# Queries, keys and layer 1's first convolution as two streams in the two column halves of TensorE's array

## What is computed

```python
# layer 0, with xn = groupnorm(x), 32 groups
f = Wq @ xn + bq          # 32 x N        g = Wk @ xn + bk          # 32 x N
h = Wv @ xn + bv          # 256 x N
beta = softmax(f.T @ g, over the first index)
x = x + gamma * (h @ beta)
# layer 1, with xn = groupnorm(x)
y = bn_relu(w1 @ xn + b1)                 # 32 channels
packed = y[rows] * y[cols]                # all 528 pairs of channels
x = x + bn_relu(w2 @ packed + b2)         # 256 x N
```

## Time and profile before

| | us |
|---|---|
| median of 3 runs | 2307.71 (2307.48 to 2309.89) |
| the profiled execution | 2308.09 |
| its span | 2305.2 |

### The profile page before, as it was taken

One profiled execution on the slowest core, in us unless ns is written; L12 is line 12 of the kernel. 1 busy time (PEld: TensorE's weight loads), 2 busy tenths in 40 slices (PEclk: granted clock), 3 DMA queues, 4 the chain that ended last, 5 costly groups with the idle time before them and its releaser, 6 DMA issues.

```text
span 2305.2 us, 42586 instructions
## 1 busy us (share of the span) xinstructions
PE 2222.7 (96%) x16782; PEld 1637.3 (71%) x16782; DVE 1891.0 (82%) x3134; ACT 1671.3 (73%) x2691; POOL 631.0 (27%) x607
## 2 busy tenths in 40 slices
PE   2899999999999999999999999999999999999978
PEld 1477777777777777777777777777777777777733
DVE  6778888888788888888888888887978777787678
ACT  3477777777777777777777777777777777777856
POOL 2100111112222332332522233333432222221244
PEclk9999999999999999999999999999999999999999
DMA  4000000000012212211122112221101111111101
GB/s 175 24 1 1 1 8 8 8 17 1 9 44 70 70 54 61 65 42 42 47 70 70 47 55 54 65 67 45 52 15 43 35 34 33 29 33 34 33 24 64
DMA packets 56663, 95.20 MB, mean 41 GB/s; under 512 B 8016, under 2 KB 14864, under 8 KB 56464
## 3 DMA queue, kind: packets, MB, share of 16 engines
q1 hardware_dynamic: 56464, 92.49, 14.1%
HBM read 67.03 MB, written 19.14 MB: 37 GB/s over the span
## 4 chain that ended last, share of the span: by engine, by line
PE 91%; DVE 6%; ACT 1%; issue 1%; SPq 0%; DMA 0%; POOL 0%; DVEq 0%; ACTq 0%
PE acc L1392 19%; PE acc L1385 19%; PE acc L1386 19%; PE tps L1235 9%; PE sps L1251 9%; PE tps L1287 3%; PE acc L1229 3%; PE tps L1289 2%; PE tps L1273 1%; PE tps L1216 1%; PE tps L1266 1%; DVE xn L593 1%; DVE mx L623 1%; PE acc L1287 1%; DVE pl L642 1%
## 5 line engine op out<-in xcount | busy, mean ns | idle before, releaser
L1028 ACT ACTIVATE ph<-sps,esc 128x512 f16<-128x512 f32 x1024 | 703.7, 687 | 397.7 <-PE sps L1251 391.8
L1385 PE MATMUL acc<-hth,ph 128*128 128x257 f16 x4096 | 955.6, 274 | 3.2 <-ACT ot L1034 3.2
L1386 PE MATMUL acc<-htl,ph 128*128 128x256 f16 x4096 | 954.8, 273 | 0.0
L623 DVE TENSOR_REDUCE mx<-tps 128x1 f32<-128x512 f32 x1024 | 700.7, 686 | 302.3 <-PE tps L1235 298.1
L642 DVE TENSOR_TENSOR pl<-p,ph 128x512 f16<-128x512 f32 x1024 | 807.2, 788 | 39.5 <-ACT p L1029 38.4
L1029 ACT ACTIVATE p<-sps,esc 128x512 f32<-128x512 f32 x1024 | 700.1, 684 | 0.0
L1392 PE MATMUL acc<-hth,pl 128*128 128x257 f16 x4096 | 620.2, 273 | 0.0
L1392 PEld LDWEIGHTS acc<-hth,pl 128*128 128x128 f16 x4096 | 399.9, 98 | 159.4 <-issue 0.3
L1386 PEld LDWEIGHTS acc<-htl,ph 128*128 128x128 f16 x4096 | 401.0, 98 | 150.7 <-issue 0.3
L876 POOL TENSOR_TENSOR xl<-xn,xh 128x512 f16<-128x512 f32 x176 | 229.8, 1327 | 877.0 <-DVE xn L593 871.2
L1385 PEld LDWEIGHTS acc<-hth,ph 128*128 128x128 f16 x4096 | 401.2, 98 | 73.8 <-issue 4.6
(11 more groups left out here) (215 smaller groups left out, 1626.7 us busy)
## 6 DMA issues: line engine op xcount, KB each, us to landing
rt<-turned SPq DMA_DIRECT2D x96, 256.0 KB, 4.2
xt<-x SPq DMA_DIRECT2D x36, 512.0 KB, 3.7
xb<-x SPq DMA_DIRECT2D x32, 512.0 KB, 5.1
out<-zt SPq DMA_DIRECT2D x47, 256.0 KB, 2.0
rt<-turned SPq DMA_DIRECT2D x72, 64.0 KB, 4.7
turned<-yb SPq DMA_DIRECT2D x24, 96.0 KB, 1.9
out<-fst SPq DMA_DIRECT2D x8, 256.0 KB, 2.0
out<-htl SPq DMA_DIRECT2D x8, 256.0 KB, 2.0
```

The source lines that it names most:

```text
L623: V.reduce_max(mx[:, tile, c:c + 1], tps[par][:], AX).then_inc(t_free[par], 1)
L1028: A(ph[:, u % SLOTS], sps[u % 2][:], ACT.Exp, scale=esc[:]).then_inc(ph_ok, 1)
L1385: mm(acc[j][:, 0:C + 1], w, hth[:, t], start=(t == 0), stop=False)
L1386: mm(acc[j][:, 0:C], w, htl[:, t], start=False, stop=False)
```

## The change

For samples 1 to 3 (b >= 1) of the queries and keys, and for layer 1's n < 24, the six matmuls now have 64 weight columns instead of 128. Channel half 0 goes to partitions 0 to 63 of the bank and half 1 to partitions 64 to 127, alternating: two sums over half the channels each, for the same 512 pixels. The two halves have to be added:

- Queries and keys: ScalarE copies partitions 64 to 127 with the bias to float32 `qk_half` (`qk_part_out`), VectorE adds them into the bank (`qk_add`), ScalarE makes the high part from the sum (`qk_high`), VectorE the low part (`qk_low`). The sum has queries once and keys once, so `spread` repeats them with six transfers instead of five.
- Layer 1: ScalarE copies partitions 64 to 127 to the lower half of `yb0` (`y_part_out`), VectorE adds twice (`y_add`), once for partitions 0 to 63 and once for 64 to 127, the second behind a wait for the first; ScalarE's `y_out` works from `yb0` in place.

Places in the loop, before and after, for b >= 1: first queries and keys on TensorE t = 9 to 8, copy out in turn 10, add in turn 10, `qk_high` 11 to 12, `qk_low` 11 to 12. Second: TensorE t = 21 as before, copy out and add in turn 23, `qk_high` and `qk_low` 23 to 25. Layer 1's first convolution: t = 17 and 18 to 18 alone; copy out and adds in turn 20; `y_out` 20 to 22. `pairs` for half 0: t = 12, 13, 14 to 13, 14, 15; `z_out` 16 to 17. `transposed` t = 4 and 7 to 3 and 6, with `finish` and `second_stats` one turn earlier as well. For sample 0 the group stays at t = 0, the copy out and the add are in turn 1, `qk_high` goes from 2 to 3.

```diff
@@ SP
+                if b:
+                    sp.wait_ge(qk_hi, n + 1)
+                    for row in (0, 32):
+                        sp.dma_start(fst[row:row + 32, b % 2, at], qkh0[0:32]).then_inc(fg_in[par], 16)
+                    for row in (0, 64):
+                        sp.dma_start(gst[row:row + 32, keys_at(n)], qkh0[32:64]).then_inc(fg_in[par], 16)
+                    sp.wait_ge(qk_lo, n + 1)
+                    sp.dma_start(fst[64:96, b % 2, at], qkl0[0:32]).then_inc(fg_in[par], 16)
+                    sp.dma_start(gst[32:64, keys_at(n)], qkl0[32:64]).then_inc(fg_in[par], 16)
+                    return
@@ VectorE, setup
+            V.tensor_copy(bq2[2 * CK:3 * CK, :], bqk[0:CK, :])
+            over_stats(V.tensor_copy(bq2[3 * CK:4 * CK, :], bqk[3 * CK:4 * CK, :]))
@@ VectorE
+                if b:
+                    V.tensor_tensor(qkl0[0:64], bank[0:64], qkh0[0:64], ALU.subtract).then_inc(qk_lo, 1)
+                    return
+            def qk_add(b, c, bank):
+                dve.wait_ge(qk_part, (b - 1) * NCH + c + 1)
+                V.tensor_tensor(bank[0:64], bank[0:64], qk_half, ALU.add).then_inc(qk_sum, 1)
+            def y_add(n, bank):
+                dve.wait_ge(y_part, n + 1)
+                V.tensor_tensor(yb0[0:64], bank[0:64], yb0[64:128], ALU.add).then_inc(y_sum, 1)
+                dve.wait_ge(y_sum, 2 * n + 1)
+                V.tensor_tensor(yb0[64:128], bank[0:64], yb0[64:128], ALU.add).then_inc(y_sum, 1)
-                        if J and t in (5, 8):
-                            finish(G - 1, (t - 5) // 3, 1)
+                        if J and t in (back + 1, back + 4):
+                            finish(G - 1, (t - back - 1) // 3, 1)
+                        if nxt and t == (10 if b else 1):
+                            qk_add(b + 1, 2 * (J - 3), tps[1])
-                        if nxt and t == (11 if b else 3):
+                        if nxt and t == (12 if b else 3):
                             qk_low(b + 1, 2 * (J - 3), tps[1])
+                        if b and t == 20:
+                            y_add(n, tps[1])
@@ ScalarE
+                if b:
+                    act.wait_ge(qk_sum, n - NCH + 1)
+                    A(qkh0[0:64], bank[0:64], ACT.Copy).then_inc(qk_hi, 1)
+                    return
+            def qk_part_out(b, c, bank):
...
+                A(qk_half, bank[64:P], ACT.Identity, bias=bq2[64:P]).then_inc(qk_part, 1)
+            def y_part_out(n, bank):
+                act.wait_ge(y_mm, n + 1)
+                if n:
+                    act.wait_ge(qh_ok, 5 * n)
+                A(yb0[64:P], bank[64:P], ACT.Copy).then_inc(y_part, 1)
             def y_out(n, bank):
+                if n < SHARED:
+                    act.wait_ge(y_sum, 2 * n + 2)
+                    A(yb0[:], yb0[:], ACT.Relu, bias=t1a[:], scale=s1a[:]).then_inc(y_ok, 1)
+                    return
@@ TensorE
+                if b:
+                    for w, v in ((0, xh), (0, xl), (1, xh)):
+                        for i in range(H2):
+                            last = mm(bank[64 * i:64 * i + 64], wqkT[:, w, i, 32:96], v[:, k % RING, i],
+                                      start=(w == 0 and v is xh), stop=(w == 1))
+                    last.then_inc(qk_mm, 1)
+                    return
+            def project_y_halves(n, bank):
+                slot = JOB["second", n // NCH, n % NCH] % RING
+                for w, v in ((0, xh), (0, xl), (1, xh)):
+                    for i in range(H2):
+                        last = mm(bank[64 * i:64 * i + 64], w1T[:, w, i, 0:64], v[:, slot, i],
+                                  start=(w == 0 and v is xh), stop=(w == 1))
+                last.then_inc(y_mm, 1)
+                    back = 3 if b else 4
-                        if J and t in (4, 7):
+                        if J and t in (back, back + 3):
-                        if b and nxt and t == 9:
+                        if b and nxt and t == 8:
-                        if b and n >= 1 and t in (12, 13, 14):
+                        if b and n >= 1 and t in (13, 14, 15):
-                        if b and t in (17, 18):
-                            if t == 17:
...
+                        if b and t == 18:
...
+                            project_y_halves(n, tps[1])
```

More of the change, by code:

```diff
@@ L161, in build @@
         xh_ok, xn_ok, xl_ok = sem("xh_ok"), sem("xn_ok"), sem("xl_ok")
-        qk_mm, qk_hi, qk_lo = sem("qk_mm"), sem("qk_hi"), sem("qk_lo")
+        qk_mm, qk_part, qk_sum, qk_hi, qk_lo = sem("qk_mm"), sem("qk_part"), sem("qk_sum"), sem("qk_hi"), sem("qk_lo")
         fg_in = [sem("fg_in0"), sem("fg_in1")]
@@ L264, in spreads, with spread_before @@
         def spreads(b, c):
-            return 80 * (qk_turn(b, c) + 1)
+            turn = qk_turn(b, c) + 1
+            return 80 * min(turn, NCH // 2) + 96 * max(turn - NCH // 2, 0)
+        def spread_before(b, c):
+            turn = qk_turn(b, c)
+            return 80 * min(turn, NCH // 2) + 96 * max(turn - NCH // 2, 0)
         def keys_at(G):
@@ L780, in attend @@
                             normed(("qk", b + 1, 2 * (J - 3) + 1))
+                        if b and t == 20:
+                            y_add(n, tps[1])
                         if nxt and t == 23:
+                            qk_add(b + 1, 2 * (J - 3) + 1, tps[1])
+                        if nxt and t == 25:
                             qk_low(b + 1, 2 * (J - 3) + 1, tps[1])
@@ L1018, in value_high @@
                 A(hth[:, t:t + 2, 0:C], bank[:].rearrange("p (t c) -> p t c", t=2), ACT.Copy).then_inc(h_hi, 1)
+            def qk_part_out(b, c, bank):
+                n = b * NCH + c
+                act.wait_ge(qk_mm, n + 1)
+                if n > NCH:
+                    act.wait_ge(qk_sum, n - NCH)
+                else:
+                    act.wait_ge(fg_in[0], spread_before(b, c))
+                A(qk_half, bank[64:P], ACT.Identity, bias=bq2[64:P]).then_inc(qk_part, 1)
[4 more added lines that the diff above has]
+                A(yb0[64:P], bank[64:P], ACT.Copy).then_inc(y_part, 1)
             def row_copy(G, bank):
@@ L1102, in attend @@
                             product_high(n - 1, (3, 4, 6, 7, 8).index(t))
-                        if nxt and t == (11 if b else 2):
+                        if nxt and t == (12 if b else 3):
                             qk_high(b + 1, 2 * (J - 3), tps[1])
+                        if nxt and t == (10 if b else 1):
+                            qk_part_out(b + 1, 2 * (J - 3), tps[1])
+                        if b and t == 20:
+                            y_part_out(n, tps[1])
+                        if nxt and t == 23:
+                            qk_part_out(b + 1, 2 * (J - 3) + 1, tps[1])
                         if b and t == 12:
@@ L1108, in attend @@
                             high(("qk", b + 1, 2 * (J - 3) + 1))
-                        if b and n >= 1 and t == 16:
+                        if b and n >= 1 and t == 17:
                             z_out(n - 1, 0, tps[1])
-                        if b and t == 20:
+                        if b and t == 22:
                             y_out(n, tps[1])
-                        if nxt and t == 23:
+                        if nxt and t == 25:
                             qk_high(b + 1, 2 * (J - 3) + 1, tps[1])
@@ L1404, in attend @@
                                     pe.wait_ge(qk_lo, (b + 1) * NCH + 2 * (J - 3) + 1)
-                            for grp in ((0, 1), (2, 3), (4,))[t - 12]:
+                            for grp in ((0, 1), (2, 3), (4,))[t - 13]:
                                 pairs(n - 1, 0, grp, tps[1])
-                        if b and t in (17, 18):
-                            if t == 17:
-                                free(1)
-                                if n >= 1:
-                                    pe.wait_ge(z_ok, 2 * n - 1)
-                                pe.wait_ge(xl_ok, JOB["second", b - 1, J] + 1)
-                            project_y(n, t - 17, tps[1])
+                        if b and t == 18:
+                            free(1)
+                            if n >= 1:
+                                pe.wait_ge(z_ok, 2 * n - 1)
+                            pe.wait_ge(xl_ok, JOB["second", b - 1, J] + 1)
+                            project_y_halves(n, tps[1])
                         if nxt and t == 21:
                             if b:
-                                pe.wait_ge(y_ok, n + 1)
+                                pe.wait_ge(y_sum, 2 * n + 2)
                             pe.wait_ge(qk_lo, (b + 1) * NCH + 2 * (J - 3) + 1)
```

34 lines of the change are left out of this document (18 added, 16 removed).

## The result

The changed kernel takes 2333.77 us (median of 4 runs, 2330.14 to 2334.73) where the kernel before takes 2308.80 beside it: 1.0105 times as long, 95% interval 1.0087 to 1.0122. It is slower by 25.0 us. The profiled execution took 2333.31 us with a span of 2331.4, 26.2 longer than the span before.

A forecast was written before the change was run, and what follows sets the result against it. TensorE's streaming columns were taken as the bound, with nothing lost to waits within a chunk. Terms -31.0 + 9.6 + 16.3 + 5.8 + 4.6 + 4.3 + 0.8 + 0.3 = +10.7 gave 2318 us, 0.45% slower; range 2292 to 2334.

The forecast's parts named there:

- gain and switching: TensorE's 48 groups: two streams at once save 31.0 us; switching the array's shape costs 0.20 a group, 9.6 us.
- first queries and keys: Samples 1 and 2 running, chunks 3 to 6: step 13 loses 0.34 and 1.70 us, 8 times, +16.3 us.
- layer 1's sum: VectorE's two adds in turn 20 make maximum 20 late for piece 21, worse in chunks 2 and 7: +5.8 us.
- transposes earlier: Turns 4 and 7 get `ql` and `finish` together: 0.11 us lost twice in 21 chunks, +4.6 us.
- second convolution later: Moved from steps 12 to 14 to 13 to 15, so step 13 starts 1.30 us earlier: +4.3 us.
- sample 0's groups: Four groups ahead of the accumulators' first matmuls, now too short to cover TensorE's wait there: +0.8 us.
- setup and both ends: Forecast for setup only: two one-column copies on VectorE in front of TensorE's first transposes, +0.3 us.
- the bound for the loads: Two weight loads of at most 117 ns per pair of streams: 0 to 0.06 us more a group, taken as 0.
- Rivals B and C: B: switching 128 to 64 columns costs nothing, 2309, chance 0.12; C: halves don't run at once, 2349, chance 0.08.
- 67.8: Sign of being right: a chunk in chunks 3 to 6 with queries and keys takes 67.8 us, from 66.84.
- 64.1: Sign of being right: a plain chunk of sample 3 takes 64.1 us, from 64.20.
- rival A: VectorE's and ScalarE's waits stay small, less than 20.3 us in all, so the kernel is faster: 2299 us, chance 0.27.

The follow-up runs named there:

- spacings: The kernel before with ten series of four VectorE additions, over same or differing partitions, put behind its last one; 2333.4 us.
- picked: The changed kernel with stalled work moved and layer 1's first convolution at full width in chunks 0, 1, 2, 7 of samples 1 and 2; 2298.72 us, 0.9957 of before.
- halves_in_turn: The changed kernel with each group's matmuls issued half by half, three of the first half of the columns, then three of the second; 2332.38 us.
- adds_apart: The changed kernel with layer 1's second add moved from VectorE's turn 20 to turn 21; 2352.0 us, 1.0188 of before.

## Why the prediction was right, and where it was short

The direction and the mechanism held: the gain is real, and the waits that it brings are larger. The size did not: forecast +10.7, measured +25.0 (spans: +26.2). 2333.77 lies 0.2 us inside the upper edge of the range, 2334, and outside the forecast's own spread of 2311 to 2330; that the time stayed in the range was luck, since the next paragraphs find one term too small by 9.9 us. By its own terms, with the sums of the step table:

| term | forecast | measured |
|---|---|---|
| gain and switching | -31.0 + 9.6 = -21.4 | 48 x 0.43 = -20.6 |
| first queries and keys | +16.3 | 8 x 2.06 = +16.5 |
| layer 1's sum | +5.8 | +15.7 |
| transposes earlier | +4.6 | 20 x 0.28 = +5.6 |
| second convolution later | +4.3 | 5 x 0.70 + 9 x 0.10 = +4.4 |
| sample 0's groups | +0.8 | 4 x 0.16 = +0.6 |
| setup and both ends | +0.3 | +3.8 |
| sum | +10.7 | +26.0 (26.2 with rounding) |

**Gain and switching.** Right, and so was the bound for the loads: pairs are 0.24 and 0.21 apart, the group takes 0.10 more going in and 0.10 more coming out. Rivals B and C are out. One reading of the prediction goes too far: the load of 96 columns in the earlier trace rows is not one of a column half and tells nothing of such loads. In the changed kernel each of the 288 loads of 64 columns takes 0.106 to 0.110 us, where the median of those with 128 is 0.098, and the two of a pair run side by side; at most the 0.02 by which the first pair is longer could be theirs.

**First group.** 2.04 forecast, 2.06 measured, through the steps named: `qk_high` late by the add, `high` behind it, `pl` 13 late, the piece of step 13 late. The inner split was off: the piece of step 11 loses 0.18, which the count did not have, and step 12 0.22 instead of 0.34. Taking away either cause gave 0.90 or 1.41, so they are not additive. That 2.04 and 2.06 agree so closely is in part two errors against each other: from the start of step 9 the add starts at 3.45 and not at 3.31, with 0.72 instead of 0.60 behind `ql`, and ScalarE's `high` follows `qk_high` after 0.49 instead of 0.58.

**Layer 1's sum: the term that was mis-sized.** The step says "the first add at 2.67, the second" at 3.40, "maximum 20 at 4.00, complete 4.69", 0.05 late (its own 4.69 and 4.61 give 0.08). Measured from the step's start at 1886.46: `pl` 21 at 2.13, adds at 2.84 and 3.56, maximum at 4.27, complete at 4.96, the piece at 5.02, 0.41 late. Of the 0.27 between 4.00 and 4.27, 0.06 is the `pl`, and 0.22 the spacing behind `pl` and ahead of the maximum: 0.60 taken, 0.71 found. It was put at 0.60 from instructions that all start at partition 0; the 0.72 in the earlier trace rows for the `pl` in front of L708, whose 32 rows start elsewhere, was the hint, and I used it at that one place only. A deadline that the count has within 0.1 us is the worst place for such an error: 15 chunks x 0.42 = 6.3, four with statistics close by 0.6 each, chunk 2 twice 1.49 instead of 1.1, chunk 7 1.84 and 1.42 plus 0.3 to 0.4 each elsewhere, instead of 1.3. Together 15.7. Chunk 7 of sample 3 loses nothing.

**Transposes** lose 0.12 + 0.12 + 0.04 for the 0.22 of the count, and nothing in the last chunk. **Moved second convolution:** 0.70 and 0.10, as counted.

**The ends.** 2.05 us of the difference lie ahead of the first chunk's third step and 1.75 behind the last scores. `spacings` has the code of before at both places. Its last matmul stands 108.6 us behind its last scores (before: 106.7, changed: 108.4), so the 1.75 need not be the change's. In front it is less clear: the third step starts at 114.81 in before and at 114.36 in `spacings`, at 116.86 in the changed kernel, and between 114.91 and 119.15 in the twelve profiles with the change in whole or in part. The two with the old setup are the earliest of fourteen, so a part of the 2.05 may be the change's; no run takes the setup apart. Windows of 20 us in the tail, about 20 to 40 us behind the last scores, of before and of `spacings`, columns as in the earlier trace rows:

```profile
2214.00:2234.00 20.00, 11.09 (x41) 3.64 (x40) 14.86 (x21) 11.25 (x18) 9.77 (x8) 0.83 0.08 28
```
```profile
2213.60:2233.60 20.00, 12.48 (x38) 3.65 (x37) 13.34 (x20) 11.16 (x17) 9.24 (x8) 0.74 0.08 28
```

The granted clock is 0.83 in one and 0.74 in the other (0.66 in the changed kernel's), that is, a larger part of the stretch at 1.2 GHz. It differs between executions of the same code. From the last scores to the end of the kernel it is 111.1 to 113.2 us in the thirteen profiles without added work, a scatter of 2 us, which the step table of the chunks does not have.

**Markers.** "67.8" for a chunk with queries and keys was 68.31, "64.1" for a plain one 64.58: both off by the spacing (0.4) and the transposes (0.1). The pairs, the 0.1 gaps and the idle of step 13 (1.7, measured 1.66) came as written. For the changed kernel rival A is out; `picked` reaches its time, because the streams are used only where they cost little.

**Still open.** TensorE: Matmul & The Clock Gate in the Trainium skill, Part 3, says matmuls start in strict program order. The 9 to 10 ns between the starts of a pair in `halves_in_turn` speak against that for column halves, though no record names an instruction's place in the program. Open too are what each of the moved places costs by itself and what the setup has of the 2.05 us in front.

## What to carry to other kernels

Where an engine is full but meets a deadline of another in every short step, a saving on it is worth only what the others can follow: lay out the other engines' queues turn by turn with spacings for exactly the kinds of instruction the change adds, and where a deadline is met by less than 0.1 us, price it from the late side. When a producer is moved, follow its consumer in the consumer's queue, as `adds_apart` did not. And choose by place: the streams lost 25 us applied everywhere and won 10 where their waits found room and with the places repaired.

## What the runs showed of the hardware that I had not expected

- VectorE: instructions of 512 columns follow each other at 0.60 us while their operands and output start at the same partitions, whole, lower or upper half alike, and at 0.70 to 0.71 at each change of start.
- TensorE: two matmuls of 64 columns in different halves, 0.22 us a pair; in the same half 0.215 each; pairs appear in the records even when the program has the halves one after the other, then with starts 9 to 10 ns apart instead of 3 to 5. Between full width and halves 0.10 us each way.
- The kernel's front scatters by some 4 us (first scores at 107.8 to 112.1 in fourteen profiles), its tail by 2, unchanged chunks by 0.03 each at most.
